# Cross-attention in a transformer layer: a batch weighed at a time, layer norm two quads ahead, Q masked in its eviction

## The reference

```python
x = x + _L0_xattn_ref(_layernorm(x), ctx, ctx, ..., Wq, Wk, Wv, Wo)   # x (32, 64, 256), ctx (32, 256, 256)
q, k, v = split_heads(xn @ Wq), split_heads(ctx @ Wk), split_heads(ctx @ Wv)   # 16 heads of 16
attn = softmax(einsum('bhqd,bhkd->bhqk', q, k))
out = einsum('bhqk,bhkd->bhqd', attn, v)   # -> (32, 64, 256)
return out @ Wo
```

## Time and profile before

| what | value |
|---|---|
| median of 3 runs | 704.86 us (702.73 to 705.59) |
| the profiled execution | 705.2 us |
| its span | 703.5 us |
| TensorE busy | 629.0 us, 89% |
| VectorE, ScalarE, GpSimd busy | 66%, 55%, 24% |
| mean granted clock of TensorE | 0.981 |
| cross-attention | from the start to 345.4 us of the span |

### The profile page before, as it was taken

One profiled execution on the slowest core, in us unless ns is written; L12 is line 12 of the kernel. 1 busy time (PEld: TensorE's weight loads), 2 busy tenths in 40 slices (PEclk: granted clock), 3 DMA queues, 4 the chain that ended last, 5 costly groups with the idle time before them and its releaser, 6 DMA issues. The chain is left out here.

```text
span 703.5 us, 18671 instructions
## 1 busy us (share of the span) xinstructions
PE 629.0 (89%) x6816; PEld 520.7 (74%) x6816; DVE 464.8 (66%) x981; ACT 384.4 (55%) x1009; POOL 169.5 (24%) x160
## 2 busy tenths in 40 slices
PE   5779588898989898997898899999999999789997
PEld 2567476777777786876587888889897988744497
DVE  3157276777777677677679975666657474657797
ACT  3157376676867677777445142433333252347895
POOL 4340515142333234150002030212112020232000
PEclk9899899999999999999999999999999999999999
DMA  7549455656564636452030000000000000000002
GB/s 239 135 127 315 111 139 121 149 134 149 130 153 113 162 86 150 103 116 62 1 120 3 2 2 1 0 0 0 0 0 0 0 2 2 2 9 0 1 31 91
DMA packets 33865, 52.09 MB, mean 74 GB/s; under 512 B 5376, under 2 KB 13696, under 8 KB 33824
## 3 DMA queue, kind: packets, MB, share of 16 engines
q1 hardware_dynamic: 29280, 42.75, 23.9%
q10 hardware_dynamic: 4352, 8.39, 4.1%
q0 software_dynamic: 192, 0.39, 0.2%
HBM read 17.96 MB, written 2.10 MB: 29 GB/s over the span
## 5 line engine op out<-in xcount | busy, mean ns | idle before, releaser
L562 ACT ACTIVATE Pr<-pS,nmax 128x256 f32<-128x256 f32 x256 | 118.9, 475 | 60.4 <-DVE nmax L658 59.4
L658 DVE TENSOR_REDUCE nmax<-pS 128x2 f32<-128x512 f32 x128 | 87.8, 687 | 76.1 <-PE pS L411 75.2
L332 POOL TENSOR_TENSOR Qst<-Qraw,rows_of 96x1024 fp32r<-96x1024 f32 x32 | 59.9, 1890 | 93.6 <-DMA Qraw<-QSh 90.8
L874 POOL TENSOR_TENSOR a_Pr<-a_Pr,a_rinv 128x512 f32<-128x512 f32 x32 | 32.7, 1044 | 185.8 <-DVE a_rinv L1163 185.8
L421 PE MATMUL pT<-ident,Pr 128*128 128x128 f32 x512 | 77.1, 272 | 0.2 <-ACT Pr L562 0.2
L411 PE MATMUL pS<-Kst,Qst 96*128 96x256 f32 x256 | 59.3, 313 | 9.9 <-ACT Pr L562 4.1
L1043 ACT ACTIVATE a_Pr<-a_Pr 128x512 f32<-128x512 f32 x32 | 20.2, 631 | 76.0 <-DVE a_Pr L1155 76.0
L421 PEld LDWEIGHTS pT<-ident,Pr 128*128 128x128 f32 x512 | 59.2, 140 | 0.4 <-ACT Pr L562 0.4
L569 ACT ACTIVATE PT<-pT 128x512 f32<-128x512 f32 x64 | 38.2, 597 | 32.1 <-PE pT L421 30.5
L411 PEld LDWEIGHTS pS<-Kst,Qst 96*128 96x128 f32 x256 | 39.4, 190 | 20.4 <-ACT Pr L562 9.0
L562 ACT ACTIVATION_READ_ACCUMULATOR Pr<-pS,nmax 128x1 f32 x256 | 52.4, 205 | 0.0
(11 more groups left out here) (266 smaller groups left out, 1880.7 us busy)
## 6 DMA issues: line engine op xcount, KB each, us to landing
Kst<-KSh SPq DMA_DIRECT2D x128, 128.0 KB, 2.5
CT<-ctxT ACTq DMA_DIRECT2D x16, 512.0 KB, 5.0
Kst<-KSl SPq DMA_DIRECT2D x64, 128.0 KB, 2.5
Qraw<-QSh SPq DMA_DIRECT2D x60, 64.0 KB, 2.0
X<-x SPq DMA_DIRECT2D x4, 512.0 KB, 8.7
out<-X SPq DMA_DIRECT2D x8, 256.0 KB, 2.2
Qraw<-QSl SPq DMA_DIRECT2D x30, 64.0 KB, 2.0
raw<-awq SPq DMA_DIRECT2D x1, 1024.0 KB, 7.3
```

Source lines behind the costliest of these rows:

```text
L332: last = pool.tensor_tensor(Qst[r][:, :, :, :, h2, :].rearrange("p j g a q -> p (j g a) q"), Qraw[:, :, r].rearrange("p j g a q -> p j (g ...
L562: act.activation(Pr[c % 2][:, t, :], pS[c % 2][:, t, :], ACT.Exp, bias=nmax[c % 2][:, t:t + 1], accum_out=rsum[par][:, c // 4, 2 * (c % 4) ...
L658: dve.tensor_reduce(nmax[s % 2][:, :], pS[s % 2][:, :, :], AX.X, ALU.max, negate=True).then_inc(maxed, 1)
```

## The change

`EVENTS` is rewritten: X at chunk 0, V at 2 and 3, Q at 4, K at 6 and 7, V at 9 and 10, K at 13 and 14. `weigh` takes a whole batch of four chunks (32 products) at chunks 1, 5, 9 and 13, each for the chunks s - 5 to s - 2, with eight PT buffers, four of which are the raw cross-attention weights' place. The steps of the output move: `turn_o` to 11 and 3, `turn_back` to 12 and 5, `project_out` to 15 and 8, with their ACT and DVE parts. Layer norm's statistics stand at chunk 4 and `normalize` at chunk 8, for two quads ahead. ACT and DVE evict Q twice, once for each column of rows_of, into a QS with one more dimension; GpSimd's queue restacks it straight into Qst, 12 DMAs for each pair, and `take_q` and Qraw are gone. The later weights are loaded one or two at a time between the K restacks of quad 0. At the start rows_of is made first, DVE splits weights before it waits for x, SP, ACT and GpSimd share the first restacks, and 12 spare products stand where 32 stood. The loop runs over one quad less, with the last but one written out.

The diff, without the declarations of semaphores, the changed wait of DVE's PT copy (the same as ACT's) and the count of spare products; "..." also leaves out unchanged lines:

```diff
-    QS = [sb(f"QS{s}", [P, 2, 2, 2, SQ], F32R) for s in "hl"]
+    QS = [sb(f"QS{s}", [P, 2, 2, 2, 2, SQ], F32R) for s in "hl"]
...
-    Qraw = sb("Qraw", [96, 4, 2, 2, 2, SQ], F32)
...
-    PT = [sb(f"PT{i}", [P, 2, KT, P], F32) for i in range(4)]
+    PT = [sb(f"PT{i}", [P, 2, KT, P], F32)[:, :, :, :] for i in range(4)]
+    PT += [wraw[:, m].rearrange("p t (k q) -> p t k q", k=KT) for m in range(4)]
...
-    EVENTS = {0: (0, "V", 1, 0), 1: (1, "X", 2, 0), 2: (2, "V", 1, 1), 3: (3, "Q", 2, 0), 5: (4, "K", 2, 0),
-              6: (5, "K", 2, 1), 8: (6, "V", 2, 0), 9: (7, "V", 2, 1), 13: (8, "K", 3, 0), 14: (9, "K", 3, 1)}
+    EVENTS = {0: (0, "X", 2, 0), 2: (1, "V", 1, 0), 3: (2, "V", 1, 1), 4: (3, "Q", 2, 0), 6: (4, "K", 2, 0),
+              7: (5, "K", 2, 1), 9: (6, "V", 2, 0), 10: (7, "V", 2, 1), 13: (8, "K", 3, 0), 14: (9, "K", 3, 1)}
...
-        with eng.Fori(1, QUADS - 1) as i:
+        with eng.Fori(1, QUADS - 2) as i:
...
+        body(QUADS - 2, False)
...
+    def two_ahead(i):
+        return not isinstance(i, int) or i + 2 < QUADS
...
-        eng.wait_ge(qraw_pool, RESTACK // 2)
-        eng.wait_ge(qraw_in, RESTACK * quads - RESTACK // 2)
-    def restack_q(eng, done, r, quads_taken, groups=range(4)):
+        eng.wait_ge(qst_in[0], RESTACK * quads - RESTACK // 2)
+        eng.wait_ge(qst_in[1], RESTACK * quads)
+    def restack_q(eng, done, par, r, chunks_done, groups=range(4)):
...
-        after(eng, q_taken, 2 * quads_taken)
+        after(eng, scores, chunks_done)
+        apart(eng, waited)
...
             for u, part in enumerate((HI, LO, HI)):
-                eng.dma_start(Qraw[32 * u:32 * u + 32, jj],
-                              f32(QS[part][32 * jj:32 * jj + 32])).then_inc(done, 16)
+                eng.dma_start(f32(Qst[par][32 * u:32 * u + 32, jj]),
+                              f32(QS[part][32 * jj:32 * jj + 32, par])).then_inc(done, 16)
+    def restack_k(eng, b, r, chunks_done, groups=range(4)):
+        after(eng, lo, r + 1)
+        apart(eng, waited)
+        after(eng, scores, chunks_done)
+        for jj in groups:
+            for u, part in enumerate((HI, HI, LO)):
+                eng.dma_start(f32(Kst[b][32 * u:32 * u + 32, jj:HP:4, :]),
+                              f32(KS[part][32 * jj:32 * jj + 32, :, :])).then_inc(kst_in[b], 16)
...
-        def restack_k(b, r, chunks_done):
-            after(sp, lo, r + 1)
-            apart(sp, waited)
-            after(sp, scores, chunks_done)
-            for jj in range(4):
-                for u, part in enumerate((HI, HI, LO)):
-                    sp.dma_start(f32(Kst[b][32 * u:32 * u + 32, jj:HP:4, :]),
-                                 f32(KS[part][32 * jj:32 * jj + 32, :, :])).then_inc(kst_in[b], 16)
-        restack_k(0, 1, 0)
-        restack_q(sp, qraw_in, 3, 0, (2, 3))
-        restack_k(1, 7, 0)
-        for m, w in enumerate(later_weights):
+        def load_later(m):
+            w = later_weights[m]
...
+        restack_k(sp, 0, 1, 0, (0, 1, 2))
+        restack_q(sp, qst_sync, 0, 3, 0, (0, 1))
+        restack_k(sp, 1, 7, 0)
...
+            first = isinstance(i, int) and i == 0
             if not last:
-                restack_q(sp, qraw_in, EV0 + EV * i + 3, i + 1)
-                restack_k(0, EV0 + EV * i + 5, CHUNKS * (p + 1))
-                restack_k(1, EV0 + EV * i + 9, CHUNKS * (p + 2))
+                if first:
+                    load_later(0)
+                restack_k(sp, 0, EV0 + EV * i + 5, CHUNKS * (p + 1))
+                if first:
+                    load_later(1)
+                    load_later(2)
+                restack_k(sp, 1, EV0 + EV * i + 9, CHUNKS * (p + 2))
+                if first:
+                    load_later(3)
...
-        def take_q(r, quad, chunks_done):
-            q_restacked(pool, quad + 1)
-            after(pool, scores, chunks_done)
-            for h2 in range(2):
-                last = pool.tensor_tensor(
-                    Qst[r][:, :, :, :, h2, :].rearrange("p j g a q -> p (j g a) q"),
-                    Qraw[:, :, r].rearrange("p j g a q -> p j (g a) q"),
-                    rows_of[0:96, h2:h2 + 1].unsqueeze(2).unsqueeze(3).to_broadcast([96, 4, 4, SQ]), ALU.mult)
-                if h2 == 0:
-                    last.then_inc(q_half, 1)
-            last.then_inc(q_taken, 1)
-        rstd_of(0)
...
-        restack_q(pool, qraw_pool, 3, 0, (0, 1))
-        take_q(0, 0, 0)
+        rstd_of(0)
+        rstd_of(1)
+        restack_q(pool, qst_in[0], 0, 3, 0, (2, 3))
...
-        take_q(1, 0, 0)
+        restack_q(pool, qst_in[1], 1, 3, 0)
         def body(i, last):
-            if not (isinstance(i, int) and i == 0):
-                take_q(1, i, CHUNKS * 2 * i)
-            if not last:
-                rstd_of(i + 1)
...
-                take_q(0, i + 1, CHUNKS * (2 * i + 1))
+            if two_ahead(i):
+                rstd_of(i + 2)
+            if not last:
+                restack_q(pool, qst_in[0], 0, EV0 + EV * i + 3, CHUNKS * (2 * i + 1))
...
+                restack_q(pool, qst_in[1], 1, EV0 + EV * i + 3, CHUNKS * (2 * i + 2))
...
                 for g in range(2):
-                    last = split_matmul(pe, bank[:, 256 * g:256 * g + 256], weights(0, slice(P * g, P * g + P)),
-                                        parts(XT))
+                    last = split_matmul(pe, bank[:, :].rearrange("p (r g n) -> p r g n", r=2, g=2)[:, :, g, :],
+                                        weights(0, slice(P * g, P * g + P)), parts(XT))
...
-                pe.wait_ge(q_taken, 2 * i + s // 8 + 1)
+                if isinstance(i, int) and i == 0 and s == 0:
+                    pe.wait_ge(qst_sync, RESTACK // 2)
+                pe.wait_ge(qst_in[par], RESTACK * (i + 1 + s // 16) - (0 if par else RESTACK // 2))
...
-            par, c = s // 8 % 2, s % 8
-            b = c // 4
-            pe.wait_ge(pt_even, 8 * i + s // 2 + 1)
-            pe.wait_ge(pt_odd, 8 * i + s // 2 + 1)
-            if c == 0:
+            par, b = s // 8 % 2, s // 4 % 2
+            pe.wait_ge(pt_even, 8 * i + s // 2 + 2)
+            pe.wait_ge(pt_odd, 8 * i + s // 2 + 2)
+            if b == 0:
...
-            for k in range(KT):
-                for n in range(4):
-                    t = n % 2
-                    j = 2 * (c % 4) + n
-                    last = pe.matmul(pO[32 * (j % 4):32 * (j % 4) + 32, j // 4, b, :, :],
-                                     V[par][:, KT * b + k, 32 * j:32 * j + 32], PT[(s + n // 2) % 4][:, t, k, :],
-                                     start=(k == 0), stop=(k == KT - 1), skip_group_check=True)
-            last.then_inc(pv_done, 2)
+            for g in range(2):
+                for k in range(KT):
+                    for n in range(4):
+                        j = 4 * g + n
+                        last = pe.matmul(pO[32 * n:32 * n + 32, g, b, :, :],
+                                         V[par][:, KT * b + k, 32 * j:32 * j + 32],
+                                         PT[(s + j // 2) % 8][:, j % 2, k, :],
+                                         start=(k == 0), stop=(k == KT - 1), skip_group_check=True)
+            last.then_inc(pv_done, 4)
...
+                if s % 4 == 1 and not (first and s == 1):
+                    weigh(i, s - 5, last)
...
-                if s % 2 == 0 and not (first and s == 0):
-                    weigh(i, s - 2, last)
-                if s == 10 or (s == 2 and not first):
-                    turn_o(2 * i + (s - 10) // 8)
-                if s == 12 or (s == 4 and not first):
-                    turn_back(2 * i + (s - 12) // 8)
-                if s == 14 or (s == 6 and not first):
-                    project_out(2 * i + (s - 14) // 8)
+                if s == 11 or (s == 3 and not first):
+                    turn_o(2 * i + (s - 11) // 8)
+                if s == 12 or (s == 5 and not first):
+                    turn_back(2 * i + (s - 12) // 7)
+                if s == 15 or (s == 8 and not first):
+                    project_out(2 * i + (s - 15) // 7)
         steps(pe, body)
-        weigh(QUADS - 1, 14, True)
+        weigh(QUADS - 1, 12, True)
...
-        if kind == "Q":
-            return (QS[s_][:, :, :, :, :].rearrange("p r g a q -> p g r (a q)"), "p (g r n) -> p g r n",
-                    dict(g=2, r=2))
...
+    def q_target(s_, h2):
+        return QS[s_][:, :, :, :, h2, :].rearrange("p r g a q -> p (r g a) q")
...
+            elif kind == "Q":
+                for h2 in range(2):
+                    last = act.activation(q_target(HI, h2), bank[:, :].rearrange("p (n q) -> p n q", q=SQ), ACT.Copy,
+                                          scale=rows_of[:, h2:h2 + 1])
+                last.then_inc(hi, 1)
...
-            after(act, pv_done, 16 * i + s - 2)
-            act.activation(PT[s % 4][:, :, :, :], pT[s % 2][:, :, :, :], ACT.Copy).then_inc(pt_even, 1)
+            after(act, pv_done, 16 * i + s - 7)
```

(53 more changed lines are left out.)

10 lines of the change are left out of this document (5 added, 5 removed).

## The result

The kernel with the change takes 671.97 us (median of four runs, 668.18 to 674.18), the kernel before, run beside it, 703.80 us (701.41 to 705.59): a ratio of 0.9545, with a 95% interval of 0.9519 to 0.9572. The forecast was 661 us in a range of 650 to 682. The time lies in the range and the direction was right. The gain is 32 us where 44 were forecast. Of the executions behind this document one, of the version with the Q part alone, took 995.79 us at a mean granted clock of 0.558 and is left out of that version's time.

The account below looks back on a forecast made before the run. TensorE, busy 89% of the span, bounds the kernel, so time comes from its gaps: start 7.7, quad 0 10.6, quads 1 to 6 24.1, last quad 1.5, sum 43.9 us; 705.2 - 43.9 = 661 us, range 650 to 682.

Parts of the forecast that it names:

- The steady quad: One quad of cross-attention away from start and end: from 36.62 us to 33.3 us, lower bound 31.9 us.
- All four waits: TensorE's idle in a steady quad before XN transposes, V projection, weighing and score: 1.28, 0.91, 0.61, 0.52 us, to go.
- the wait for On: New TensorE wait at chunk 12, before outputs are transposed back, for On from DVE: 1.1 us a quad.
- 0.3 us for CS low: New wait of the K projections for GpSimd's CS low: 0.3 us a quad, between 0 and 2.4.
- The changeovers of weighing: Four fewer changeovers from weighing 32 products four times: 0.1 us each, 0.4 us a quad, bounds 0 and 1.
- The rival built on slow issues: GpSimd's queue becomes the bound: slower from 1.42 us an issue on, 736 us at 1.6 us; chance 0.06.
- the two terms counted: At the start, ahead of Q: K low about 1.6 us earlier, Q low 0.3 us earlier than 22.88 + 0.69.
- the price of the K stack: Pair 0's K restack, ready about level with TensorE at chunk 14: no cost, upper bound 1 us a quad.
- the other two signs of being wrong: GpSimd issues taking over 1 us, or the clock falling in more than two quads.
- The 1 us for the later weights: In quads 1 to 6, 2 MB of weights ahead of the second K restack cost 1 us in all.
- new waits take half: Rival: score, maximum, exponential chain has little slack at light chunks; quads 34.5 to 36 us, 669 to 680 us; chance 0.22.
- the quad does not shrink: Rival: the two other engines set the quad at 36.6 us, only start and quad 0 gain, 687 us; chance 0.04.

Follow-up runs that it names:

- the version with the Q part alone: Kernel before plus only Q masked in two evictions on ScalarE and VectorE and restacked by GpSimd's queue, old schedule kept: 696.58 us (median of three), ratio 0.9890.

## Why the prediction was right, and where its size was off

**The steady quad: right, its number partly by luck.** 33.0 to 33.4 us against 33.3. All four waits went, the wait for On came at chunk 12 with 0.83 + 0.25 = 1.1 us as forecast, and 0.3 us for CS low was hidden behind the unforeseen wait for Kst until the latter was removed. But two misses cancel in the sum. It had 1.15 us less busy time (four drains and four changeovers less one new drain), and the busy time fell by 1.72 (33.31 to 31.59); it had 2.2 us less idle time, and that fell by 1.73. The changeovers of weighing, 0.4 us with a bound of 1, were the term put too low, and the wait for Kst was the term put at nothing.

**GpSimd's queue: right.** 24 issues a quad at 0.50 us (0.51 forecast), landing in 2.1 us, 17.4 us of work a quad (17.8 forecast):

```profile
L271 POOL DMA_DIRECT2D Qst<-QSh x124 | 62.0, 503 | 13.7 <-DVE QSl L649 6.9
```

DVE is busy for 26.7 of 33.2 us beside them. The Trainium skill (page "SBUF — State Buffer", section "SBUF: two separate sides") gives about 3.1 us for a DMA from GpSimd that overlaps a DVE copy in a two-port mode. Neither the issues (0.50 us) nor the landings (2.1 us) show that here. Whether any DVE operation of this kernel ran in such a mode no row shows, so this does not speak against the page. The rival built on slow issues fell.

**The start: right in kind, 2.1 us better,** 9.8 us gained against 7.7 with bounds of 5 and 9. From the first GpSimd issue on it went as forecast: 3.2 us of issues and 3.2 us to the score. But that issue came at 21.53 and not at 23.7. Q low was out at 20.79, where the prediction had 0.3 us less than 23.57. The chain ahead of Q had been shortened by more than the two terms counted.

**What failed: the price of the K stack.** The step reads "Level; today this wait shows now and then … Nothing, with 1 us a quad as the upper bound", and ahead of it "DMA share from 0.56 to about 0.7 … No queue waits by that alone". Both are off in the same way. The step priced one of two stacks. It took the one with its issues in the way at chunk 14, and left out that of pair 1, due at chunk 6, though the schedule's shortening lies ahead of chunk 6. And it took a mean share over a quad. The mean came out at 0.71, as forecast, but the 11.7 us in which pair 1's stack is in flight stand at 0.96. The 1 us a quad as upper bound held in the steady quads (0.57 to 0.94 us) and not over the run, where 16.6 us came in eight quads. The sign that was to tell of it, a wait at chunk 14 in every quad, did not come, since it watched the other stack; nor did the other two signs of being wrong. That the transfers there are the cause is shown from three sides: fewer bytes in the stretch remove the wait (context load at chunk 6), the same bytes from two queues don't, and bytes moved onto the other stack make that one late.

**The 1 us for the later weights** was the same mistake at its largest. In quad 1 the weights (share 1.09 in the window below) held the stack back for 4.77 us, and the clock added 2.6. Moving them took 6.7 us off. The sum took it that no quad would meet a low clock, and named 3 us for two that do. It was two quads, 4.1 us, both with a long wait, and neither met a low clock where its wait was under 1 us (quad 1 with the weights in the last quad, quad 5 with the second context load at chunk 6 as well). That the wait is all it takes is not shown; the last section has a quad that lost clock without a long one.

```profile
78.00:86.00 8.00, 3.23 (x46) 2.63 (x46) 3.59 (x7) 3.60 (x11) 6.18 (x9) 0.82 1.09 260
```

**The rivals.** The 661 us stood for 654 to 668 us, with a chance of 0.60, and the time is not in there. It lies in the 669 to 680 us of the rival "new waits take half" (0.22), and so does the mean of quads 0 to 6, 35.15 us, in its 34.5 to 36. It is there not for that rival's reason: the chain of score, maximum and exponential kept its slack. So the range held because it took in this rival whole. The rival "the quad does not shrink" was mispriced, without effect: its 687 us take the full 10.6 us for quad 0, where a quad of 36.6 us gives 7.3, so some 690. With the transfers out of the way the span is 655.4 us, 4.2 less than the forecast span of 659.6, with a start of 31.8, quads 1 to 6 of 197.7 (200.8 forecast) and 2.5 us given back in the last quad.

## What to carry to other kernels

When a schedule is tightened, list for each transfer from when to when it is in flight and when it is due in the new order, and take the DMA share of just that stretch. A mean of 0.7 over the loop says nothing of a stretch at 0.96, and all stacks must be priced, not the one that waited before. Where the transfers don't fit, move one whose due time is far, and look at what it lands beside; adding an issuing queue helps only while it is the issuing that is late. A wait of about 3 us or more cost another half of itself through the clock here, and once nearly as much again (1.6 us on 2.96, 2.6 on 4.77, 1.9 to 3.2 on 3.4), so two rare long waits can outweigh a short one in every round.
